# A convolution tile shared by three engines: every second chunk on ACT and POOL

## The reference

```python
def _path(x, w1, b1, ..., m3, v3):            # one of 32 paths
    h = relu(bn1(x @ w1 + b1))                # 64 -> 4 channels
    h = relu(bn2(conv3x3(h, w2) + b2))        # 4 -> 4 channels
    return relu(bn3(h @ w3 + b3))             # 4 -> 64 channels
y = relu(sum_over_paths(_path(x)) + x)
z = (y - mean(y)) / sqrt(var(y) + 1e-5)       # then q, k, v = z @ W_qkv.T
```

## Time and profile before

| | us |
|---|---|
| median of 3 runs | 6784.15 |
| the profiled execution's own time | 6765.31 |
| its span | 6763.6 |
| convolution: first and last tile start on DVE | 147.0, 1490.4 |

### The profile page before, as it was taken

How to read it: one execution, slowest core, us unless ns; L and a number is a source line. 1 busy time by engine, 2 the same in 40 slices (tenths; PEclk the granted TensorE clock), 3 DMA queues, 4 the chain that set the end, 5 groups by cost and what they waited for, 6 DMA issues and landing times. The chain is left out here.

```text
span 6763.6 us, 59936 instructions
## 1 busy us (share of the span) xinstructions
PE 3366.5 (50%) x16368; PEld 2375.4 (35%) x16368; DVE 3733.1 (55%) x5332; ACT 962.3 (14%) x1813; POOL 3137.9 (46%) x2752
## 2 busy tenths in 40 slices
PE   2788878767888888845444400572222222222000
PEld 0344434336777777734333300341111111111000
DVE  4988888857999999942999400321111111111129
ACT  0112222212333333312000000110000000000000
POOL 0000000003333333312888777677777777777545
PEclk9878787768988989855555555555555555555555
DMA  6455555542222222233100100121111111111125
GB/s 136 81 85 86 85 85 85 84 71 65 63 60 61 60 60 61 60 84 76 31 8 8 20 8 4 56 79 32 32 32 32 32 32 32 30 30 28 25 71 201
DMA packets 551500, 384.17 MB, mean 57 GB/s; under 512 B 370652, under 2 KB 504572, under 8 KB 548452
## 3 DMA queue, kind: packets, MB, share of 16 engines
q1 hardware_dynamic: 357724, 237.30, 13.2%
q10 hardware_dynamic: 116200, 116.30, 9.1%
q0 software_dynamic: 77472, 29.41, 4.4%
HBM read 235.03 MB, written 147.68 MB: 57 GB/s over the span
## 5 line engine op out<-in xcount | busy, mean ns | idle before, releaser
L1406 POOL DMA_INDIRECT e_row<-scratch_table,e_edge x2048 | 2232.4, 1090 | 704.8 <-issue 670.7
L1584 PE MATMUL f_psY<-f_w,f_hid 128*128 128x64 f32 x1568 | 347.3, 423 | 1835.1 <-ACT f_hid L1535 1835.1
L1584 PEld LDWEIGHTS f_psY<-f_w,f_hid 128*128 128x128 f32 x1568 | 338.1, 332 | 1909.9 <-ACT f_hid L1535 1784.6
L1486 DVE TENSOR_TENSOR e_e<-e_row,e_b 128x512 f32<-128x512 f32 x16 | 11.3, 704 | 1321.1 <-DMA e_row<-scratch_table,e_edge 1320.9
L902 POOL TENSOR_TENSOR q_exp<-q,a_headmask 64x1792 f32<-64x1792 f32 x112 | 361.1, 3224 | 798.7 <-DMA q<-scratch_q 798.7
L895 POOL MEMSET val<- 100x1792 f32 x2 | 3.1, 1592 | 1527.6 <-POOLq L137 1527.6
L765 DVE SCALAR_TENSOR_TENSOR acc<-psE,c_b,acc 128x448 f32<-128x448 f32 x840 | 569.0, 677 | 105.7 <-PE psE L458 89.1
L1444 DVE TENSOR_TENSOR i_hot<-i_iota,i_digit 128x1024 bf16<-128x1024 f32 x512 | 581.4, 1207 | 9.5 <-DMA i_before<-in_before 9.5
L964 PE MATMUL psO<-prob_t,val 100*128 100x128 f32 x3136 | 457.3, 296 | 185.2 <-DVE own L1042 185.2
L458 PE MATMUL psE<-stack,c_w 72*128 72x448 bf16 x896 | 387.7, 450 | 308.1 <-DVE acc L765 179.4
L445 PE MATMUL psH<-h,c_w 128*128 128x448 f32 x1008 | 534.2, 618 | 0.9 <-ACT h L548 0.9
(11 more groups left out here) (269 smaller groups left out, 5195.1 us busy)
## 6 DMA issues: line engine op xcount, KB each, us to landing
stack<-scratch_parts ACTq DMA_DIRECT2D x504, 112.0 KB
val<-scratch_vpad SPq DMA_DIRECT2D x1120, 35.0 KB
e_row<-scratch_table,e_edge POOLq DMA_INDIRECT x2048
scratch_y<-f_y ACTq DMA_DIRECT2D x49, 512.0 KB, 2.9
g_y<-scratch_y SPq DMA_DIRECT2D x28, 896.0 KB, 4.9
scratch_state<-e_state SPq DMA_DIRECT2D x16, 1536.0 KB, 6.0
scratch_parts<-h2p ACTq DMA_DIRECT2D x56, 336.0 KB, 2.2
keys<-scratch_kpad SPq DMA_DIRECT2D x112, 155.0 KB
```

What stands on the lines that cost most here:

```text
L1406: pool.indirect_dma_start(out=row[s][:, f, :], out_offset=None, in_=table_dram, in_offset=bass.IndirectOffsetOnAxis(ap=edge[s][:, 0, f:f + ...
L1584: m = pe.matmul(psY[par][:, j, e * C:(e + 1) * C], hid[e][:, j * 128:(j + 1) * 128], w2[:, e, :], start=True, stop=True)
```

## The change

- ACT reads the odd chunks: `lift` takes psE with Relu and the bias pos3 into one of three buffers `lifted` (float32, 128x448). DVE accumulates the even chunks alone. POOL adds the eight lifted chunks up in acc2 (seven additions, `sum_lifted`) and adds acc2 to acc (`merge`); `to_tokens` waits for the merge.
- psE has three banks; psT shares psQK's, so `z_to_channels` waits for the q and k of the tile before to have been read.
- `rest` and `last_part` go from DVE to POOL, behind POOL's waits for the first and second lift; center, square and scale of the layernorm go to POOL too. The six steps left on DVE stand behind chunks 2, 4, 6, 10, 12 and 15.
- ACT's order is new: lifts stand between its other steps, h2_relu goes ahead of qkv, and its loop over images is written out.

```diff
-        psE = [ps(f"psE{i}", [128, 512]) for i in range(2)]
+        psE = [ps(f"psE{i}", [128, 512]) for i in range(3)]
         psTurn = ps("psTurn", [128, 512])
         psQK = ps("psQK", [128, 512])
+        psT = psQK
         psFV = ps("psFV", [128, 512])
...
+                def rest(n, t):
+                    g = n * TILES + t
+                    pool.wait_ge(part_done[0], g + 1)
+                    wait(pool, split_done, g)
+                    pool.tensor_tensor(h2r[:], h2[:, SLOT[t]], h2p[:, SLOT[t], 0], ALU.subtract).then_inc(rest_done, 1)
+
+                def last_part(n, t):
+                    g = n * TILES + t
+                    pool.wait_ge(part_done[1], g + 1)
+                    pool.tensor_tensor(h2p[:, SLOT[t], 2], h2r[:], h2p[:, SLOT[t], 1], ALU.subtract).then_inc(split_done, 1)
+
+                def sum_lifted(n, t, k):
+
+                    g = n * TILES + t
+                    at = g * EACH + k
+                    pool.wait_ge(lift_done, at + 1)
+                    if k == 0:
+                        return
+                    wait(pool, sum_done if k > 1 else acc_done, at if k > 1 else g)
+                    first = lifted[:, (at - 1) % 3] if k == 1 else acc2[:]
+                    m = pool.tensor_tensor(acc2[:], first, lifted[:, at % 3], ALU.add)
+                    m.then_inc(sum_done, 2 if k == 1 else 1)
+
+                def merge(n, t):
+                    g = n * TILES + t
+                    pool.wait_ge(stt_done, (g + 1) * EACH)
+                    pool.wait_ge(sum_done, (g + 1) * EACH)
+                    pool.tensor_tensor(acc[:, SLOT[t]], acc[:, SLOT[t]], acc2[:], ALU.add).then_inc(acc_done, 1)
+
+                def center(n, t):
+                    g = n * TILES + t
+                    pool.wait_ge(meaned, g + 1)
+                    wait(pool, z_done, g)
+                    pool.tensor_tensor(cen[:], t1[:, t], stat[:, t, 1].unsqueeze(2).to_broadcast([TOK, SUB, C]), ALU.add).then_inc(centered, 1)
+                    pool.wait_ge(centered, g + 1)
+                    pool.tensor_tensor(sq[:], cen[:], cen[:], ALU.mult).then_inc(squared, 1)
+
+                def scale(n, t):
+                    g = n * TILES + t
+                    pool.wait_ge(inverted, g + 1)
+                    pool.tensor_tensor(z[:, t], cen[:], stat[:, t, 5].unsqueeze(2).to_broadcast([TOK, SUB, C]), ALU.mult).then_inc(z_done, 1)
+
+                def tile(n, t, first, last):
+                    sum_lifted(n, t, 0)
+                    if not last:
+                        rest(*ahead(n, t, 1))
+                    sum_lifted(n, t, 1)
+                    if not last:
+                        last_part(*ahead(n, t, 1))
+                    sum_lifted(n, t, 2)
+                    sum_lifted(n, t, 3)
+                    if not first:
+                        center(*ahead(n, t, -1))
+                    for k in range(4, EACH):
+                        sum_lifted(n, t, k)
+                    merge(n, t)
+                    if not first:
+                        scale(*ahead(n, t, -1))
+
+                rest(0, 0)
+                last_part(0, 0)
+                for n in range(N):
+                    for t in range(TILES):
+                        tile(n, t, n == 0 and t == 0, n == N - 1 and t == TILES - 1)
+                center(N - 1, TILES - 1)
+                scale(N - 1, TILES - 1)
...
                     for c in range(CHUNKS):
-                        wait(pe, stt_done, g * CHUNKS + c - 1)
-                        pe.matmul(psE[c % 2][:, 0:PIX], w3[:, c, :], stack[SLOT[t]][:, c, :],
+                        at = g * CHUNKS + c
+                        wait(pe, lift_done if (at - BANKS) % 2 else stt_done, (at - BANKS) // 2 + 1)
+                        pe.matmul(psE[at % BANKS][:, 0:PIX], w3[:, c, :], stack[SLOT[t]][:, c, :],
...
-                    pe.wait_ge(stt_done, (g + 1) * CHUNKS)
+                    pe.wait_ge(acc_done, g + 1)
...
-                    wait(pe, zt_done, g)
+                    wait(pe, qk_done, g)
...
+                def lift(n, t, c):
+                    at = (n * TILES + t) * CHUNKS + c
+                    act.wait_ge(e_ready, at + 1)
+                    wait(act, sum_done, at // 2 - 2)
+                    act.activation(lifted[:, at // 2 % 3], psE[at % BANKS][:, 0:PIX], ACT.Relu, bias=pos3[:, c:c + 1])\
+                       .then_inc(lift_done, 1)
...
                             h1_relu(*ahead(n, t, 3))
+                        lift(n, t, 1)
                         if not (last and t + 1 >= TILES):
                             second_part(*ahead(n, t, 1))
+                        lift(n, t, 3)
+                        if not (last and t + 1 >= TILES):
                             store_parts(*ahead(n, t, 1))
                         if not (first and t == 0):
                             relu(*ahead(n, t, -1), first)
+                        lift(n, t, 5)
                         if not (first and t <= 1):
                             turned(*ahead(n, t, -2))
+                        lift(n, t, 7)
                         if not (last and t + 1 >= TILES):
                             stack_parts(*ahead(n, t, 1))
+                        lift(n, t, 9)
+                        lift(n, t, 11)
+                        if not (last and t + 2 >= TILES):
+                            h2_relu(*ahead(n, t, 2))
+                        lift(n, t, 13)
                         if not (first and t <= 1):
                             qkv(*ahead(n, t, -2), first)
-                        if not (last and t + 2 >= TILES):
-                            h2_relu(*ahead(n, t, 2))
+                        lift(n, t, 15)
...
+                        dve.tensor_scalar(st(1), st(0), -1.0 / C, None, ALU.mult).then_inc(meaned, 1)
+
+                    def squares():
+                        dve.wait_ge(squared, g + 1)
+                        dve.tensor_reduce(st(2), sq[:], AX.X, ALU.add).then_inc(ln_step, 1)
+
...
-                    return [residual, total, minus_mean, center, square, squares, variance, inverse, scale]
+                    return [residual, total, minus_mean, squares, variance, inverse]
...
-                        dve.wait_ge(e_ready, g * CHUNKS + c + 1)
-                        if c == 0:
-
-                            dve.tensor_scalar(acc[:, SLOT[t]], psE[0][:, 0:PIX], b3[:, 0:1], sumb3[:, 0:1], ALU.max, ALU.add)\
-                               .then_inc(stt_done, 1)
-                        else:
-                            dve.wait_ge(stt_done, g * CHUNKS + c)
-                            dve.scalar_tensor_tensor(acc[:, SLOT[t]], psE[c % 2][:, 0:PIX], b3[:, c:c + 1], acc[:, SLOT[t]],
-                                                     ALU.max, ALU.add).then_inc(stt_done, 1)
-                        if c % 2 == 0 and c >= 2 or c >= 14:
+                        if c % 2 == 0:
+                            at = g * CHUNKS + c
+                            dve.wait_ge(e_ready, at + 1)
+                            if c == 0:
+
+                                wait(dve, acc_done, g - 1)
+                                dve.tensor_scalar(acc[:, SLOT[t]], psE[at % BANKS][:, 0:PIX], b3[:, 0:1], sumb3[:, 0:1], ALU.max, ALU.add)\
+                                   .then_inc(stt_done, 1)
+                            else:
+                                dve.wait_ge(stt_done, at // 2)
+                                dve.scalar_tensor_tensor(acc[:, SLOT[t]], psE[at % BANKS][:, 0:PIX], b3[:, c:c + 1], acc[:, SLOT[t]],
+                                                         ALU.max, ALU.add).then_inc(stt_done, 1)
+                        if c in LN_AT:
```

More of the change, by code:

```diff
@@ L126 @@
 STACK = 9 * 2 * DP
-REST_AT, LAST_PART_AT = 0, 3
+LN_AT = (2, 4, 6, 10, 12, 15)
 SORT_SLOTS = (4, 5, 6, 7, 8, 9, 10, 11, 12)
@@ L274, in conv_phase @@
         b3 = sb("c_b3", [128, CHUNKS])
+        pos3 = sb("c_pos3", [128, CHUNKS])
         sumb3 = sb("c_sumb3", [128, 1])
@@ L290, in conv_phase @@
         acc = sb("acc", [128, 3, PIX])
+        lifted = sb("lifted", [128, 3, PIX])
+        acc2 = sb("acc2", [128, PIX])
         usum = sb("usum", [TOK, SUB, C])
@@ L329, in conv_phase @@
         c_ready = sem("c_ready"); h2_done = sem("h2_done")
-        e_ready = sem("e_ready"); stt_done = sem("stt_done")
+        e_ready = sem("e_ready"); stt_done = sem("stt_done"); lift_done = sem("lift_done"); sum_done = sem("sum_done"); acc_done = sem("acc_done")
+        centered = sem("centered"); squared = sem("squared"); inverted = sem("inverted"); meaned = sem("meaned")
         f_ready = sem("f_ready"); u_done = sem("u_done"); t1_done = sem("t1_done")
@@ L352, in conv_phase @@
         HC = 2 * DP
+        EACH = CHUNKS // 2
+        BANKS = len(psE)
         with nc.Block() as block:
@@ L490, in project @@
                     pe.wait_ge(zt_done, g + 1)
-                    wait(pe, qk_done, g)
```

(18 more changed lines are left out.)

6 lines of the change are left out of this document (removed).

## The result

The changed kernel takes 6974.72 us (median of 4 runs, 6968.27 to 6983.77) against 6782.76 for the kernel before in the same runs: ratio 1.029, 95% interval 1.0269 to 1.0311. The prediction was 7008 with a range of 6895 to 7110.

A forecast was written before the change was run, and what follows sets the result against it. Bound: a DMA cycle through the stack transfer, DVE nearly as high. Tile 10.4 + 17.5 + 0.6 = 28.5 us; 55 periods add 224 to 6765.3, giving 6989; the median's 18.8 above makes 7008 us, range 6895 to 7110.

The forecast's parts named there:

- Two bounds of nearly the same height: Convolution tile: the DMA cycle through the stack transfer and DVE's work, the first not lowered by taking work off DVE.
- Ten microseconds less on DVE bought nothing: Tile 52, past the sort: DVE busy 14.1 of 24.15 us, yet as long as the mean tile, 24.43.
- DVE's 7.9 us: Accumulates, splits and layernorm steps taken off DVE per tile; beside the DMA cycle, so costed at nothing.
- A = 10.4: Offset in us of a tile's first stack DMA from S, DVE's first accumulate; before 6.4, range 9.2 to 11.5.
- X = 17.5: Length in us of the stack transfer, from its first DMA until landed, ahead of PE's next chunk 0.
- X unchanged: Sign to look for: the stack transfer keeps its length, taken as 17.5 us.
- Its length goes with its 1.03 MB: Stack transfer: its time follows its bytes, as DMA share is 0.59 with nothing else of size under way.
- T = 28.5: Convolution tile period in us: first stack DMA's offset 10.4, plus transfer 17.5, plus 0.6 to DVE's next start.
- stage +224: Convolution's 55 tile periods: 1567 us against 1343, so 224 us longer.
- the one chain that matters: Steps from tile start to first stack DMA: the change's added POOL sum, slower splits and lifts cost 4.0 us a tile.
- The shared port: Rival: DVE's min/max steps and POOL's sums exclude each other; tile about 30.5 us, +335, 7119 us; chance 0.13.
- all fit: Other engine work per 28.5 us tile: ACT 14.3, POOL 13.3, DVE 15.8, PE 21.1, so none binds.

The follow-up runs named there:

- e5: Kernel before, with parts stored in three DMAs and the stack loaded by three DMAs of 24 rows instead of nine of 8: ratio 0.9897 to before.
- e4: Changed kernel, with parts stored in three DMAs and the stack loaded by three DMAs of 24 rows, same bytes: ratio 1.018 to before.
- e1: Changed kernel with the splits rest and last_part back on DVE at their old places: ratio 1.0183 to before.
- e2: Changed kernel with the nine stack DMAs ahead of lift 7 in ACT's queue instead of behind it: ratio 1.0256 to before.
- e3: Changed kernel with both edits, splits back on DVE and stack DMAs ahead of lift 7: ratio 1.0047 to before.
- e8: Changed kernel with splits still on POOL but a tile earlier, parts store and stack DMAs moved ahead in ACT's queue: ratio 1.0126 to before.
- e7: e4 with six of POOL's seven sums a tile shrunk from 448 columns to 8, waits kept: ratio 0.997 to before.
- e11: Kernel before with splits on POOL in their own loop, stack in three DMAs of 24 rows, and center, square and scale on POOL: ratio 0.9783 to before.

## Why the prediction was right, step by step

- *Two bounds of nearly the same height.* Shown by e5: with a shorter transfer the tiles behind the sort fall by 5.6 us, the sorted ones by 0.6. Which bound holds depends on the tile: in the kernel before, the 15 tiles with nine min and max steps are 25.24 us long, and in 13 of them the transfer had landed 0.2 us or more before PE's chunk 0; they were DVE's. "Ten microseconds less on DVE bought nothing" set tile 52 against the mean of all tiles, 24.43; against the full ones, those behind the sort (24.55) are 0.7 shorter. The 59 waits of the earlier trace rows count weight loads and matmuls each. DVE's 7.9 us bought nothing in the changed kernel: its busy share between 300 and 1400 us is 678.7/1100 = 0.62, forecast near 0.6, and the tile is 4 us longer.
- *A = 10.4.* Measured 9.52, most often 9.2. Each price was a little high: lift 0.63 (0.70), POOL's splits 1.03 (1.13), the lifts' start S+1.78; so the store at 6.95 instead of 7.75. And what came last was the landing of the parts, some 2.25 us behind the store, in 51 of 55 tiles, not ACT's queue, which I had at 2.65. In eight of 55 tiles the store was out only at 8.2: there `to_tokens` waited 0.92 us for POOL's merge, and chunk 1 came later.
- *X = 17.5.* Measured 18.34, above the 17.9 that I took as its upper end, though tile 27 alone already had 18.1. "X unchanged" failed: by the landings the transfer grew from 16.7 to 18.2, and nearly all of it in the sorted tiles (16.6 to 18.3; behind the sort 17.4 to 17.7). SP's q store starts 11.8 us (median) after the first stack DMA, before 15.2, so more of the transfer has company. But within neither trace does the length follow that start (correlation -0.2 and -0.1), so this cause is argued, not shown. "Its length goes with its 1.03 MB" is refuted by e4 and e5, where the same bytes land in 8.8 and 8.2 us.
- *T = 28.5, stage +224.* 28.45 and +221.9. The two errors, -0.9 and +0.8, cancel: that the sum is better than its terms is luck.
- *The step that I put too simply* is "puts a POOL sum, two slower splits and four lifts into the one chain that matters". There were two chains, ending 0.5 us apart: the splits' (parts landed at S+9.2) and that of lift 7 (begun at S+8.67 in the median; in tile 32 at 1071.60, with PE's chunk 7 done at S+8.5). I had the second at 8.9 + 0.7 and counted it as slack. e1 and e2, each without one of them, gain 1.5 and 0.4 us; e3, without both, gains 3.3.
- *The shared port.* A rival with 0.13; as a mechanism it is there (1.5 to 1.6 us for steps of 1.2), and 38 of 48 tiles with such steps have one of 2 us or more. Of its second sign, a to_tokens that waits for the merge, there is little: it waited in ten of 55 tiles, and in the sorted tiles the merge had ended 2.4 us before it on average. So "all fit" held in most tiles, and by e8's bound of 26.8 with 1.8 us to spare in the mean of the sorted ones; in the tiles with nine steps (28.4) there was nothing to spare. The Trainium skill ("SBUF — State Buffer", on the shared port pair) says that the loser fully blocks; the lengths of POOL's sums, 1.62 on average against 1.13 alone, agree, as does e7. My price for the rival, 30.5 in each full tile, was too high: only one period of 55 is above 30, and where the merge does hold every tile those with nine steps take 28.4 (e8) and 29.8 (e4).
- *The transfer.* The Trainium skill ("DMA: Bandwidth & Descriptors", "Why a DMA increments its semaphore by 16 and not by 1") has a DMA spread over the largest number of engines up to 16 that divides the slowest dimensions; by that, 24 rows use 12 engines where 8 rows use 8. The trace agrees in direction: the DMA share in the middle of the transfer goes up from 0.58 to 0.85, as these windows of 1 us of the changed kernel and of e4 show, both behind the sort (length, busy us by engine, PEclk, DMA share, GB/s).

```profile
1616.00:1617.00 1.00, 1.00 (x4) 0.47 (x3) 0.14 (x2) 0.86 (x2) 0.86 (x2) 1.00 0.58 53
...
1568.00:1569.00 1.00, 1.00 (x4) 0.47 (x3) 0.13 (x2) 0.85 (x2) 0.89 (x1) 1.00 0.85 147
```

The length falls from 18.2 to 8.8 us, by more than the factor 8 to 12. There are also three DMAs instead of nine; how much is due to that was not tested.
- *The other signs.* PE's idle time ahead of chunk 0, forecast at 5 us or more, was 4.5 on average and 5 or more in 22 of 55 tiles; POOL's sums were at 1.62, not 1.1.
- *Medians.* 192 us against 218 in the profiled executions: the profiled one of before, 6765, was 17 below its median, the one after, 6984, was 9 above. That is most of why the forecast of 7008 lies 33 us above the median, while that of the stage was 2 us off; of a change of 192 us it is a sixth.

## To carry to other kernels

Before you move work to an idle engine, look at what it will stand behind there. The two splits cost 1.5 us a tile behind a lift and a sum, and gained 1.0 on the same engine in a queue of their own. When tiles with ten microseconds less work on the busiest engine are hardly shorter than the full ones (24.55 and 25.24 here), look for a cycle through a transfer, and tell the kinds of tiles apart before you take a mean; shorten the way to its first DMA or the transfer, and treat every wait put ahead of it, in each queue, as time added to every tile. Two chains that end close together hide each other: undo both before you call either harmless.

## What the runs showed of the hardware

- POOL's split with a bf16 operand takes 1.03 us, less than its float32 sum of two tensors, 1.13.
- In e11, POOL's center and square of 256 columns took 1.22 and 1.23 us between 300 and 1300 us, and 0.61 alone, while DVE's min and max steps stayed at 1213 ns. In the changed kernel, with 13 and mostly longer POOL operations a tile instead of 5, both sides grew (1.46 to 1.64, and 1.62 for the sums).
- The same 1.03 MB, loaded as three blocks of 24 rows instead of nine of 8, landed in 8.8 us instead of 18.2 (e4), and in 8.2 instead of 16.7 (e5). Its price is on ACT's queue: three stores take 1.84 us there, one 0.35.
- ACT's queue starts a DMA that stands behind a lift when the lift has begun, and does not wait for its end (0.01 us behind the start in the median of e1).
